# First block of an AdaLN transformer kernel: q and k rounded once per batch and spread over the heads by one-pass matmuls, with x and the weights loaded from two queues, and a new table of places for both blocks

## The reference, cut to what matters

```python
x = L0_attn_x                                    # 4 x 512 x 128
mod = (silu(c) @ wmod).reshape(4, 6, 1, -1)
h = layernorm(x) * (1 + ca) + sa
# first block
ct_q = h @ Wd_q_w; ct_kv = h @ Wd_kv_w           # 64 columns each
query = heads(ct_q @ Wu_q_w) + heads(rope(ct_q @ Wq_r_w))
key = heads(ct_kv @ Wu_k_w) + heads(rope(h @ Wk_r_w))
value = heads(ct_kv @ Wu_v_w)
attn = softmax(einsum('bhqd,bhkd->bhqk', query, key) / scale)
x = x + ga * (einsum('bhqk,bhkd->bhqd', attn, value) @ Wo_w)
# second block
h = layernorm(x) * (1 + cb) + sb
for i in range(6):
    h = attn_layer(shift_tokens(h), ...) + h     # q, k of length 1, rotary, softmax in a window, @ Wo
    h = ffn_layer(shift_tokens(h), ...) + h      # layernorm, (h @ W1a) * gelu(h @ W1g) @ W2
x = x + gb * h
```

## Time and profile before

| | us |
|---|---|
| median of 3 runs (least to most) | 1966.91 (1966.37 to 1968.31) |
| the profiled execution: time, span | 1975.51, 1973.7 |
| PE, DVE, ACT, POOL busy in the span | 1808.0, 1682.5, 1190.9, 1272.3 |
| mean granted TensorE clock | 0.99 of full speed |

### The profile page before, as it was taken

The page is one execution under the profiler, slowest core; times in us unless marked ns, Lnnn a source line. Parts: engine busy times, 40 slices in busy tenths (PEclk is TensorE's granted clock), DMA queues, the critical chain, the costliest instruction groups (busy, mean ns, idle before and its releaser), DMA issues.

```text
span 1973.7 us, 49730 instructions
## 1 busy us (share of the span) xinstructions
PE 1808.0 (92%) x19284; PEld 1227.4 (62%) x19284; DVE 1682.5 (85%) x2794; ACT 1190.9 (60%) x2134; POOL 1272.3 (64%) x1650
## 2 busy tenths in 40 slices
PE   6999999789989999999999999999999999999986
PEld 2444444366666666666666676666666666676764
DVE  3777786799889989898999899998999899989982
ACT  1455566456666566656665666666656665666654
POOL 5112012577678777777876887767877778777761
PEclk9999999899999999999999999999999999999998
DMA  2000001345455555555555555545564546455552
GB/s 57 1 1 6 6 1 55 104 167 178 151 171 177 173 164 165 175 165 165 172 177 165 169 171 178 181 144 182 163 195 156 169 157 194 161 182 163 179 163 66
DMA packets 189287, 274.87 MB, mean 139 GB/s; under 512 B 23358, under 2 KB 85372, under 8 KB 188924
## 3 DMA queue, kind: packets, MB, share of 16 engines
q1 hardware_dynamic: 189052, 271.69, 42.4%
HBM read 71.33 MB, written 52.43 MB: 63 GB/s over the span
## 4 chain that ended last, share of the span: by engine, by line
DVE 37%; PE 34%; issue 10%; POOL 10%; ACT 8%; DMA 0%; SPq 0%; POOLq 0%; DVEq 0%; ACTq 0%
DVE turned L931 11%; DVE kz L951 11%; PE psum L558 4%; DVE rd L967 3%; PE psum L774 3%; PE psum L614 3%; PE psum L735 3%; POOL u L1313 3%; PE psum L637 3%; PE psum L560 2%; PE psum L559 2%; PE psum L746 2%; PE psum L714 2%; DVE smax L958 2%; PE psum L628 2%
## 5 line engine op out<-in xcount | busy, mean ns | idle before, releaser
L931 DVE SCALAR_TENSOR_TENSOR turned<-psum,vecs,tabs 128x1024 f32<-128x1024 f32 x384 | 487.9, 1271 | 18.4 <-POOL u L1313 6.8
L1108 ACT ACTIVATE sq<-psum 128x512 f32<-128x512 f32 x384 | 226.2, 589 | 112.3 <-PE psum L560 112.2
L1302 POOL TENSOR_TENSOR sdiff<-sdiff,rqs 128x512 f32<-128x512 f32 x192 | 201.1, 1047 | 126.9 <-DVE sdiff L963 121.2
L1313 POOL TENSOR_TENSOR qT<-turned,swapped 128x512 f32<-128x512 f32 x192 | 242.8, 1287 | 52.9 <-PE psum L714 50.7
L951 DVE TENSOR_TENSOR kz<-u,psum 64x512 f32<-64x512 f32 x384 | 259.4, 675 | 4.0 <-PE psum L702 0.7
L1313 POOL TENSOR_TENSOR u<-turned,swapped 128x512 f32<-128x512 f32 x192 | 242.1, 1282 | 14.6 <-DMA swapped<-turned 14.4
L1286 POOL TENSOR_TENSOR px<-px,rd 128x512 f32<-128x512 f32 x192 | 201.4, 1049 | 73.1 <-DVE rd L969 73.0
L558 PE MATMUL psum<-xs_hi,wqk_hi 128*128 128x512 f32 x384 | 183.6, 478 | 61.0 <-DVE turned L931 60.3
L735 PEld LDWEIGHTS psum<-pxT,v 128*64 128x64 f32 x6144 | 194.7, 138 | 69.5 <-issue 63.3
L735 PE MATMUL psum<-pxT,v 128*64 128x64 f32 x6144 | 221.2, 225 | 1.9 <-DMA pxT<-scratch 1.0
L746 PEld LDWEIGHTS psum<-onT,wo 128*128 128x128 f32 x1536 | 197.1, 191 | 21.4 <-issue 7.0
(11 more groups left out here) (182 smaller groups left out, 3710.2 us busy)
## 6 DMA issues: line engine op xcount, KB each, us to landing
swapped<-turned SPq DMA_DIRECT2D x384, 256.0 KB, 2.5
scratch<-pt SPq DMA_DIRECT2D x192, 256.0 KB, 2.2
pxT<-scratch SPq DMA_DIRECT2D x384, 128.0 KB, 2.9
v<-v SPq DMA_DIRECT2D x192, 192.0 KB, 2.5
w_raw<-in_wqkv SPq DMA_DIRECT2D x36, 256.0 KB, 3.1
v<-v SPq DMA_DIRECT2D x144, 64.0 KB, 2.2
wo<-in_wo SPq DMA_DIRECT2D x12, 256.0 KB, 3.3
w_raw<-in_w SPq DMA_DIRECT2D x12, 170.5 KB, 2.7
```

Source lines behind the costliest of these rows:

```text
L931: engine.scalar_tensor_tensor(out=turned[:, n % NROT, :, :], in0=both, scalar=vec(("ks" if which else "qs", i)), in1=tabs[:, 2 * which:2 * ...
L1108: engine.activation(sq[:, n % NSQ, :], bank(n % 2), ACT.Square).then_inc(s_sq, 1)
L1302: engine.tensor_tensor(sdiff[:, :, :], sdiff[:, :, :], r_, ALU.mult).then_inc(s_weigh, 1)
L1313: engine.tensor_tensor(u[:, n % GT, :] if which else qT[:, m_, :], turned[:, n % NROT, 0, :], swapped[:, n % NSWAP, :], ALU.add).then_inc( ...
```

## The change

1. **pack.** q and k of a batch are rounded once (`qk_hi`, ScalarE) and the rest is taken once (`qk_lo`, VectorE), in the new step `parts`. `selg` becomes four sets of 0/1 matrices in fp32r (128 x 2048 in place of 128 x 512), and a pack is two one-pass matmuls into one bank. ScalarE alone drains it. VectorE's step `pack` and the tiles `lam`, `hi`, `qkT`, `yT` go.
2. **Loads.** x comes batch by batch, each with its own semaphore. Ten weights are issued from ScalarE's queue and have the semaphore `s_a`; `selg` is loaded as float32 into `pT` and copied to fp32r by GpSimd. SP issues the rest in a new order. What had waited for all of x or for all weights waits for its own part; TensorE's and VectorE's `rope` and GpSimd's copy of `selg` wait for all ten.
3. **Places.** `mod` gets places of its own behind x's transposes and moments. `AFTER, UNIT, EARLY` and every row of `PLACES`, the table of the second block, are changed.

```diff
+    "mod": dict(tensor=-10.5, vector=-11.8, scalar=-14.0),
+    "parts": dict(vector=-7.9, scalar=-8.0),
-    "pack": dict(tensor=-6.2, vector=-6.0, scalar=-6.0, gpsimd=-5.4),
+    "pack": dict(tensor=-6.2, scalar=-6.0, gpsimd=-5.4),
...
-AFTER, UNIT = 33.3, 0.69
-EARLY = 11.1
+AFTER, UNIT = 33.5, 0.98
+EARLY = 5.7
...
-    "norm_rows": dict(tensor=1.35, scalar=1.25),
+    "norm_rows": dict(tensor=1.2, scalar=1.2),
...
-    "product": dict(tensor=3.35, vector=3.5),
+    "product": dict(tensor=3.7, vector=4.2),
...
# TensorE
             elif kind == "pack":
                 b, n, g = k
-                pe.wait_ge(s_qk, nth_a["qk", b, n])
+                pe.wait_ge(s_selg, 1)
+                pe.wait_ge(s_qk_lo, nth_a["parts", b, n])
                 pe.wait_ge(*bank_a.free(*step))
-                engine.matmul(bk, selg[:, g, :], qkT[:, b % 2, n, :], start=True, stop=True).then_inc(fills, 1)
+                engine.matmul(bk, selg[:, n, 0, g, :], qk_hi[:, n, :], start=True, stop=False)
+                engine.matmul(bk, selg[:, n, 1, g, :], qk_lo[:, n, :], start=False, stop=True).then_inc(fills, 1)
...
# VectorE
+            elif kind == "parts":
+                b, n = k
+                dve.wait_ge(s_qk_hi, nth_a[step])
+                engine.tensor_tensor(qk_lo[:, n, :], rot[:, 0, :], qk_hi[:, n, :].bitcast(F32), ALU.subtract).then_inc(s_qk_lo, 1)
...
-            elif kind == "pack":
-                b, n, g = k
-                dve.wait_ge(s_hi, nth_a[step])
...
-                engine.scalar_tensor_tensor(out=k_all[:, g % 2, :] if n else q3[b % 2][:, g, :], in0=hi[:, :].bitcast(F32),
-                                            scalar=lam[:, n:n + 1], in1=bk, op0=ALU.mult, op1=ALU.add).then_inc(empties, 1)
...
# ScalarE
+            elif kind == "parts":
+                b, n = k
+                act.wait_ge(s_qk, nth_a[step])
+                if b:
+                    act.wait_ge(*bank_a.full("pack", b - 1, n, NG - 1))
+                engine.copy(qk_hi[:, n, :], rot[:, 0, :]).then_inc(s_qk_hi, 1)
...
-                engine.activation(hi[:, :], bk, ACT.Identity, bias=onesc[:, 0:1] if n else 0.0).then_inc(s_hi, 1)
+                if n:
+                    engine.activation(k_all[:, g % 2, :], bk, ACT.Identity, bias=onesc[:, 0:1]).then_inc(empties, 1)
+                else:
+                    engine.copy(q3[b % 2][:, g, :], bk).then_inc(empties, 1)
...
# GpSimd
+        pool.wait_ge(s_a, 16 * 10)
+        engine.tensor_copy(selg[:, :, :, :, :].rearrange("p n w g m -> p (n w g m)"), selg_raw).then_inc(s_selg, 1)
...
# SP
+        engine.dma_start(x0[:, 0:TT, :], a["x"][0].rearrange("(t p) d -> p t d", p=P)).then_inc(s_x[0], 16)
...
-        engine.dma_start(x0[:, :, :], a["x"].rearrange("b (t p) d -> p (b t) d", p=P)).then_inc(s_x, 16)
...
+        for b in range(1, B):
+            engine.dma_start(x0[:, b * TT:(b + 1) * TT, :], a["x"][b].rearrange("(t p) d -> p t d", p=P)).then_inc(s_x[b], 16)
```

More of the change, by code:

```diff
@@ L155, in order_a @@
             put(8 * b + 0.8 * n, "qk", b, n)
+            put(8 * b + 0.8 * n, "parts", b, n)
         for g in range(NG):
@@ L168, in order_a @@
                     put(place + half + c / 2, "weighted", b, g, half, c)
-    start = [(-20.0, ("mod",))] * (engine in ("tensor", "vector", "scalar"))
-    return start + [(place, step) for place, _, step in sorted(timed)]
+    return [(place, step) for place, _, step in sorted(timed)]
 def tile(n):
@@ L188 @@
                                                  ("w1", 1)))
-AFTER, UNIT = 33.3, 0.69
-EARLY = 11.1
+AFTER, UNIT = 33.5, 0.98
+EARLY = 5.7
 START, UP = 7.6, 0.0
 PLACES = {
[L198 to L204, removed]
-    "norm_rows": dict(tensor=1.35, scalar=1.25),
[L206 to L215, removed]
-    "product": dict(tensor=3.35, vector=3.5),
[L217 to L222, removed]
-    "up": dict(tensor=7.9, vector=8.05),
-    "down": dict(tensor=9.1, vector=9.7),
-    "write_out": dict(tensor=11.1, vector=10.1, scalar=11.45, sync=12.3),
@@ new lines @@
+    "shift_parts": dict(vector=0.1, gpsimd=0.1),
+    "heads": dict(tensor=-0.1, vector=0.55, scalar=0.1),
+    "swap": dict(sync=0.65),
+    "rotate": dict(gpsimd=1.65),
+    "square_sums": dict(tensor=0.05, scalar=0.35),
+    "norms": dict(tensor=0.55, vector=0.7, scalar=1.0),
+    "norm_parts": dict(gpsimd=1.1),
+    "norm_rows": dict(tensor=1.2, scalar=1.2),
+    "scale": dict(tensor=3.3, vector=3.5),
+    "mask": dict(scalar=-0.9),
+    "weigh": dict(gpsimd=0.0),
+    "scores": dict(tensor=-0.35, vector=-0.15, scalar=0.4),
@@ new lines @@
+    "prob_sums": dict(vector=0.7, gpsimd=0.7),
+    "blocks": dict(vector=1.25),
+    "move": dict(sync=1.5),
+    "fetch": dict(sync=1.95),
+    "values": dict(tensor=1.6, scalar=1.95, gpsimd=1.0, sync=1.7),
+    "apply": dict(tensor=2.9, scalar=3.0),
+    "product": dict(tensor=3.7, vector=4.2),
+    "shifted": dict(scalar=4.15),
+    "token_major": dict(tensor=5.35, scalar=5.45),
+    "statistics": dict(vector=5.7, gpsimd=6.2),
+    "scaled": dict(scalar=6.4),
+    "feature_major": dict(tensor=7.6, scalar=7.85, gpsimd=7.45),
@@ L226 @@
+    "gate": dict(tensor=8.15, scalar=8.05),
+    "up": dict(tensor=8.25, vector=8.35),
+    "down": dict(tensor=8.85, vector=9.4),
+    "write_out": dict(tensor=11.6, vector=11.35, scalar=11.55, sync=12.0),
 }
@@ L438, in build @@
     s_const = sem("s_const_loaded")
-    s_x = sem("s_x_loaded")
+    s_x = [sem(f"s_x{b}_loaded") for b in range(B)]
+    s_c, s_down = sem("s_c_loaded"), sem("s_wd_loaded")
     s_a = sem("s_weights_a_loaded")
@@ L1487, in constants @@
     c["ropes"] = np.ascontiguousarray(np.repeat(np.sin(r), 2, axis=1).T * sgn[:, None])
-    selg, onesc = np.zeros((P, NG, P), f), np.zeros((P, 1), f)
-    lam = np.zeros((P, 2), f)
-    for g in range(NG):
-        for h in range(AG):
-            for k in range(3):
-                for d in range(AD):
-                    selg[(AG * g + h) * AD + d, g, 32 * h + AD * k + d] = 1
-    for h in range(AG):
-        onesc[32 * h + 3 * AD, 0] = lam[32 * h + 3 * AD, 1] = 1
-        lam[32 * h + 2 * AD:32 * h + 3 * AD, 0] = -1
-        lam[32 * h + AD:32 * h + 2 * AD, 1] = -1
-    c.update(selg=selg, onesc=onesc, lam=lam)
+    selg, onesc = np.zeros((P, 2, 2, NG, P), f), np.zeros((P, 1), f)
+    blocks = (((0, 1), (2,)), ((0, 2), (1,)))
+    for g, h, d, n, part in itertools.product(range(NG), range(AG), range(AD), range(2), range(2)):
+        for k in blocks[n][part]:
+            selg[(AG * g + h) * AD + d, n, part, g, 32 * h + AD * k + d] = 1
+    onesc[3 * AD::32, 0] = 1
+    c.update(selg=selg, onesc=onesc)
     half = np.arange(0, DH, 2, dtype=f)
```

96 lines of the change are left out of this document (49 added, 47 removed).

## The result

The changed kernel takes 2035.16 us (median of 4 runs, 2033.55 to 2049.6), the kernel before beside it 1966.64: a ratio of 1.0363 (95% interval 1.0315 to 1.0411). It is 68.5 us slower; 1922 had been forecast, in a range of 1892 to 1957. The profiled execution took 2033.55 us.

The account below looks back on a forecast made before the run. TensorE was taken to bound the first block, TensorE and VectorE, both nearly full, the second. Pack -13, loads 0 and table -32 sum to -45 us: 1922 us on the median of 1966.9, range 1892 to 1957.

Parts of the forecast that it names:

- The pack, -13 us: First block: cheaper packs save TensorE 14 us, a new cast and subtraction chain costs 1; ends 0 and -20.
- The loads, 0 us (-1.5 to +1.2): Start: x lands sooner, but `rstd` stays behind GpSimd's copy of `selg`, starting between 14.1 and 16.8 us.
- The table, -32 us: Second block: new order shortens VectorE's waits by 53 us, six tenths taken; ends 0 and -53.
- work, which no order removes: Second block: nine tenths of both engines' time, cited for the rival that the table does nothing (1954 us).
- the rivals: Pack alone, 1954 us (0.22); slower, 1987 us (0.10); all waits go, 1901 us (more than 1895: 0.06); no change (0.04).
- `rd`: Second block: VectorE's `rd` waits less for ScalarE's exponential `px`, as `norm_rows` stands behind apply; -28 us.
- product: Second block: VectorE takes scores and a tile of `turned` before TensorE's product, which is then ready; -20 of 23 us.
- `up`: Second block: `rq` comes sooner, so the ScalarE chain behind it starts up to 0.2 us sooner, 24 times; -5 us.
- The rival of TensorE at `norm_rows`: Second block: TensorE stands 1.2 us, 48 times, for `rn` behind apply, 58 us; slower, 1987 us; chance 0.10.
- my sign of being wrong: Second block: the table forecast is wrong if TensorE shows waits for `rn` of over 0.8 us each.
- Six tenths of 53 us: Second block: share of the table's summed wait savings taken to come through, -32 us.
- joints (±5): Last 15 tiles of heads before the first scores, the change of block and the program's end: 0, plus or minus 5 us.

Follow-up runs that it names:

- the runs with the gap: Changed kernel plus a one-column fill on GpSimd behind its own `xs_lo`, VectorE's order untouched: 1970.58 us.
- with the constants: Changed kernel, `shift_parts` ahead of the scores, plus an unused VectorE operation on constant tiles behind them, 23 times: subtraction 2042.85 us, reduction 1970.16 us.
- With `xs_lo` mended: Changed kernel with one table number altered, putting VectorE's `shift_parts` ahead of its unit's scores again: 1967.93 us.
- a single move: New first block, old table, `shift_parts` directly behind the reciprocal (1957.91 us), plus TensorE's `norm_rows` moved right behind apply: 1961.29 us.
- The two mended tables: Old table: new first block, `shift_parts` behind the reciprocal, `selg` copy behind `rstd`, 1949.7 us. New: changed kernel, `shift_parts` ahead, clear behind `weigh`, same copy move, 1950.48.
- the one move of the clear: Changed kernel with `shift_parts` ahead of the scores (1967.93 us), plus GpSimd's clear of `v` moved behind `weigh`: 1961.45 us.
- the run of 1949.7 us: New first block, old table, `shift_parts` directly behind the reciprocal (1957.91 us), plus GpSimd's `selg` copy moved behind the first `rstd`: 1949.7 us.

## Why the prediction was wrong, step by step

**The pack, -13 us: right in place and about in size.** A pack in the changed kernel (TensorE's timeline):

```profile
156.37 0.39 PE L614 MATMUL psum<-qk_hi,selg 128*128 128x512 f32 x1
156.60 0.40 PE L615 MATMUL psum<-qk_lo,selg 128*128 128x512 f32 x1
156.84 0.39 PE L622 MATMUL psum<-k_odd,q_odd 128*128 128x512 f32 x1
```

From the first to what follows it are 0.47 us, against the 0.46 of the working. The first block ends 11.4 us sooner (338.2 against 349.6), with `rstd` 2 us later. To the end 7 to 8 us arrive; where the rest went was not traced. Pack and loads were not run apart, so how the 11.4 us divide between them stays open.

**The loads, 0 us (-1.5 to +1.2): mis-sized.** The copy of `selg` took 1.89 us, not 2.4, but its wait ended at 15.38, not by 14.4 as I had worked out from 290 GB/s, and `rstd` came at 17.37 us, 1.8 us later than in the earlier trace rows and outside of my range. That what x gains is hidden behind this copy was right; I did not see how much it is. With the copy out of the way 8 us come out.

**The table, -32 us: the step that failed.** By the runs the table costs 67 + 6 = 73 us. It failed twice. First, I counted only waits. Of VectorE's own operations I took it that an order neither removes nor adds to them ("work, which no order removes"), and the price of each was read from the old order. The order does add: it decides whether `xs_lo` meets GpSimd's row of operations. The run that moves this one step back gives 67 of the 68.5 us, and the runs with the gap and with the constants show what makes them: VectorE's 64-row subtraction waits out GpSimd's row, 3.85 us on average and over 5 us in 13 of 24 cases, for 0.69 us of work. The old trace had a sign of it that I passed over: `xs_lo` took 1.44 us for 64 rows where a pass over twice the rows takes 0.69, and GpSimd's half 1.58 us. None of the rivals had it. The one on the slower side named another place.

Second, the waits themselves. With `xs_lo` mended the new table stands at 1967.9 us against 1962.3 with the old one, +6 where I had -32. For `rd` and product the waits had their causes where I said; for `up` no run shows it. For `rd` a single move took 26 us away in the stretch, near to the 28 of the working. But its time did not come through; waits for `rn`, `kz`, product and `up` came or grew instead. The rival of TensorE at `norm_rows` was near: it was to decide from a stall of 0.8 us each, and 0.76 were measured in the run of that move, with no gain left. In the changed kernel the same stall is 16.5 us in 20 waits, 0.83 us each: my sign of being wrong, but in half of the cases. Product was gone from VectorE's waits as forecast, but TensorE came to wait 16.2 us for its bank. `up`, which I had 5 us shorter, was 5 us longer, and TensorE's wait for `turned`, which was to fall, rose to 72.2 us (37.0 with `xs_lo` mended). Six tenths of 53 us was a guess at how much passes. The two mended tables, 1949.7 and 1950.5 us, say that over the whole table nothing does, though the one move of the clear did bring its 6 us.

**The range** was narrower than its own terms: the ends of pack (-20 to 0), loads (-1.5 to +1.2), table (-53 to 0) and joints (±5) give 1887 to 1973 us, not 1892 to 1957. The measured 2035 lies outside of both; no term of the sum could have made it.

**The joints, 0 ± 5:** not measured by themselves; nothing shown speaks against it.

By the runs the parts are: first block and loads -7, `xs_lo` +67, the rest of the table +6, together +66; measured are +68.5. These are steps from one kernel to the next, so their sum has to come out and checks nothing. The 2.5 us that are left are what the kernel before differs by between the two series (1966.6 and 1969.1).

## What to carry to other kernels

Before an operation of VectorE is moved, look at what GpSimd runs beside it at the new place. If both read SBUF with two inputs, or VectorE's is a scalar operation like the one tried here, price it by the length of GpSimd's row of such operations up to its next pause, fill or cast, not by the operation; put it where it starts first, as directly behind the result that releases GpSimd. An instruction that takes longer than its size says (1.44 us for a 64-row pass) may be such a wait, though it is booked as work. Waits of two engines that are both nine tenths full are not to be summed: one taken away is worth nothing until a run says so (26 us less of one gave nothing, 6 us less of another gave 6), and a copy that waits for a load belongs behind what does not need it.

## What the runs showed of the hardware

- The wait is not for one instruction. By the Trainium skill, SBUF — State Buffer, section Who interferes with whom, the one that starts first has the shared ports for its whole instruction and the other blocks. Here VectorE waited through four of GpSimd's: the rest of `xs_lo`, `weigh` and two rotations, 5.04 us for 0.69 us of work. With a fill of one column between two of them it was let in there in 21 of 24 cases (1.70 us); once it was not (2.62 us).
- Not every border between two such operations of GpSimd is closed. In the kernel before, VectorE began during `px` and got in between it and GpSimd's `xs_lo` in 21 of 24 cases, 1.48 us in all:

```profile
910.21 1.05 POOL L1286 TENSOR_TENSOR px<-px,rd 128x512 f32<-128x512 f32 x1 [1.37 <-DVE rd L969]
910.33 1.48 DVE L922 TENSOR_TENSOR xs_lo<-rT,xs_hi 64x511 fp32r<-64x511 f32 x1
911.22 1.73 POOL L1292 TENSOR_TENSOR xs_lo<-rT,xs_hi 64x512 fp32r<-64x512 f32 x1
```

  In the changed kernel it never got in between `xs_lo`, `weigh` and the rotations where they follow without a pause. But it did between `weigh` and the rotations in the rows at 1834 us above, and once in the kernel before with the step behind the scores (2.39 us). Why a border lets it in at one time and not at another is not settled.
- The mean granted clock from 400 to 1900 us was 1.00 in the kernel before, 0.98 in the changed kernel, where TensorE stands for up to 3.5 us at a time, 0.99 with `shift_parts` ahead and 1.00 in the run of 1949.7 us. What that alone cost was not measured.
